# Cross-attention with scores in 32-row groups of heads over four banks, layer norm of x on POOL and a new order of work

## What is computed

```python
x = x + _L0_xattn_ref(_layernorm(x), ctx_1024, ctx_1024, w_q, w_k, w_v, w_o)
...
# each of them, with 16 heads of 8 numbers; scale, bias and mask differ by layer
Q = (query @ w_q.T).reshape(B, L, N_HEADS, D_K).transpose(0, 2, 1, 3)
K = (key @ w_k.T).reshape(B, L, N_HEADS, D_K).transpose(0, 2, 1, 3)
V = (value @ w_v.T).reshape(B, L, N_HEADS, D_K).transpose(0, 2, 1, 3)
scores = jnp.einsum('bhqd,bhkd->bhqk', Q, K) / jnp.sqrt(jnp.float32(D_K))
attn = jax.nn.softmax(scores, axis=-1)
out = jnp.einsum('bhqk,bhkd->bhqd', attn, V)
return out.transpose(0, 2, 1, 3).reshape(B, L, D_MODEL) @ w_o.T
```

## Time and profile before

| | us |
|---|---|
| median of 3 runs | 3282.99 (3280.1 to 3283.28) |
| the profiled execution | 3285.16 |
| its span, first to last instruction | 3283.5 |
| L0 cross-attention, from its first transposes | 27 to 335 |
| L1 cross-attention | 508 to 816 |
| L2 cross-attention | 1233 to 1565 |
| L3 cross-attention | 1669 to 1974 |

### The profile page before, as it was taken

One profiled execution on the slowest core, in us unless ns is written; L12 is line 12 of the kernel. 1 busy time (PEld: TensorE's weight loads), 2 busy tenths in 40 slices (PEclk: granted clock), 3 DMA queues, 4 the chain that ended last, 5 costly groups with the idle time before them and its releaser, 6 DMA issues. The chain is left out here.

```text
span 3283.5 us, 95494 instructions
## 1 busy us (share of the span) xinstructions
PE 3036.9 (92%) x34128; PEld 2065.7 (63%) x34128; DVE 2480.1 (76%) x5721; ACT 1622.4 (49%) x2596; POOL 981.8 (30%) x1128
## 2 busy tenths in 40 slices
PE   5999678998999999999989996999997989999989
PEld 3666565666566656666656664666674656666655
DVE  6888686887677767777568877888885668888756
ACT  3666214565333334555346666666663356666523
POOL 4000000000000000000110005888882268888734
PEclk9999668999999999999899998999998999999999
DMA  4111001111000002111001110000001100000022
GB/s 155 29 30 23 13 0 24 28 30 24 7 0 0 0 5 42 40 40 23 13 20 46 40 41 14 10 10 10 10 3 26 26 14 10 6 10 10 4 77 77
DMA packets 190847, 81.12 MB, mean 25 GB/s; under 512 B 175921, under 2 KB 176496, under 8 KB 190208
## 3 DMA queue, kind: packets, MB, share of 16 engines
q1 hardware_dynamic: 187024, 69.14, 9.1%
q0 software_dynamic: 3696, 10.28, 0.9%
HBM read 37.54 MB, written 8.39 MB: 14 GB/s over the span
## 5 line engine op out<-in xcount | busy, mean ns | idle before, releaser
L864 ACT ACTIVATE probs_t<-ps_pt 128x1024 f32<-128x1024 f32 x256 | 262.2, 1024 | 388.4 <-PE ps_pt L980 388.4
L726 DVE TENSOR_REDUCE row_max<-ps_s 128x16 f32<-128x1024 f32 x256 | 313.2, 1223 | 113.5 <-PE ps_s L969 110.4
L2088 POOL TENSOR_TENSOR kblk<-kblk 128x1024 f32<-128x1024 f32 x128 | 302.1, 2360 | 140.3 <-DVE kblk L2131 140.3
L710 POOL TENSOR_TENSOR x<-x,out_bias_L 128x512 f32 (+1 forms) x32 | 40.6, 1270 | 971.9 <-DVE x_norm L495 500.8
L731 DVE TENSOR_TENSOR probs<-ps_s,row_max 128x1024 f32<-128x1024 f32 x256 | 311.9, 1218 | 11.7
L1002 PE MATMUL ps_o<-v,probs_t 128*64 128x18 f32 x8192 | 285.9, 213 | 5.4 <-issue 5.3
L1002 PEld LDWEIGHTS ps_o<-v,probs_t 128*64 128x64 f32 x8192 | 260.5, 138 | 40.4 <-issue 19.0
L980 PE MATMUL ps_pt<-ident,probs 128*128 128x128 f32 x2048 | 278.1, 279 | 7.2 <-ACT probs L859 7.2
L969 PE MATMUL ps_s<-kblk,q_t 64*64 64x512 f32 x2048 | 273.6, 607 | 5.7 <-issue 5.6
L859 ACT ACTIVATE probs<-probs 128x1024 f32<-128x1024 f32 x256 | 269.6, 1053 | 14.4 <-DVE probs L731 13.0
L1682 POOL TENSOR_TENSOR probs<-probs 128x512 f32<-128x512 f32 x16 | 16.6, 1039 | 860.9 <-ACT probs L1659 860.9
(11 more groups left out here) (334 smaller groups left out, 6823.2 us busy)
## 6 DMA issues: line engine op xcount, KB each, us to landing
ci<-in_ctx_t SPq DMA_DIRECT2D x64, 256.0 KB, 3.0
kblk<-k_t SPq DMA_DIRECT2D x688, 16.0 KB
ci<-x SPq DMA_DIRECT2D x64, 128.0 KB
ci<-x SPq DMA_DIRECT2D x128, 63.0 KB
x<-in_x_in SPq DMA_DIRECT2D x4, 1024.0 KB, 8.7
mask<-in_mask_l SPq DMA_DIRECT2D x64, 64.0 KB, 2.5
out<-x SPq DMA_DIRECT2D x16, 256.0 KB, 2.0
out<-x POOLq DMA_DIRECT2D x16, 256.0 KB, 2.4
```

The costliest lines, as they stand in the source:

```text
L726: dve.tensor_reduce(row_max[u % 2][:, :], scores_of(u), AX, ALU.max).then_inc(max_ready.sem, 1)
L864: act.activation(probs_t[:, :, :], ps_pt[:, :, :].rearrange("p a (r t) -> p (a r) t", t=P), ACT.Copy).then_inc(pt_ready.sem, 1)
L2088: pool.tensor_tensor(a, a, b_, ALU.add).then_inc(rotated.sem, 1)
```

## The change

- **Scores.** RG is 4: four groups of 32 rows (four heads each), eight matmuls of 32x64 with 256 columns for a tile. Row group c writes bank c, so that a tile takes half of each of all four banks, and scores of tile u wait for the shift of tile u - 1. The masks are put in by eight matmuls of 256 columns in place of four of 512, still with 64 rows (MASK_ROWS). maxima and shift read the same 1024 numbers, now out of four banks. kblk is half as long per group of keys; place_keys still has 16 transfers of the same size.
- **Norm.** POOL does a group with two instructions of 128x512 (x - mean, then times 1/deviation); norm_tile is gone from DVE in these stages. POOL's late loads in L0 are issued in portions of five behind each of the first groups.
- **V.** values_even is ACT's too.
- **Order.** The lists of PE, DVE and ACT are written anew.

The core of the diff; the new lists of DVE and ACT and the changed names of kblk are left out:

```diff
-RG = 2
+RG = 4
+MASK_ROWS = P // 2
...
+            score_banks = ps_s[:, :, 0:RH * S]
+            scores_4 = score_banks.rearrange("p c (h k) -> p c h k", k=S)
...
-                    if name == "L0":
-                        for dst, src in late_loads:
-                            pool.dma_start(dst, src).then_inc(loaded_late.sem, 16)
+                    late = late_loads if name == "L0" else []
+                    unrolled = 10 if late else 1
+                    share = (len(late) + unrolled - 1) // unrolled
+                    def normalise_rows(g):
...
+                        wait_past(pool, xt_in_psum, g, 0)
+                        pool.sem_inc(pool_turn.sem, 1)
+                        pool.tensor_tensor(x_norm[:, :, :], rows,
+                                           mean_all[:, bass.ds(g * GT, GT)].unsqueeze(2).broadcast_to(spread),
+                                           ALU.subtract).then_inc(x_norm_ready.sem, 1)
...
+                    for g in range(unrolled):
+                        body(g)
+                        for dst, src in late[g * share:(g + 1) * share]:
+                            pool.dma_start(dst, src).then_inc(loaded_late.sem, 16)
...
-                        wait_past(pe, shifted, g, u - 1)
+                        wait_past(pe, shifted, g, u)
                         pe.sem_inc(pe_turn.sem, 1)
-                        bank = ps_scores[u % 2]
...
                         for c in range(RG):
                             rows = slice(c * RP, (c + 1) * RP)
                             for b in range(2):
                                 tok = slice((2 * u + b) * S, (2 * u + b + 1) * S)
-                                last = pe.matmul(bank[b * S:(b + 1) * S, c, :], q_t[par][rows, tok],
+                                last = pe.matmul(score_banks[b * S:(b + 1) * S, c, :], q_t[par][rows, tok],
                                                  kblk[par][rows, :, tok], start=plain, stop=True,
                                                  skip_group_check=not plain)
```

More of the change, by code:

```diff
@@ L1025, in body @@
                         if soon:
-                            project_v(g + 1, other)
-                            scores(g + 1, 0, other)
+                            scores(g + 1, 0, 1 - par)
+                        if late:
+                            project_k(g + 2, par)
                         if now:
```

151 lines of the change are left out of this document (77 added, 74 removed).

## The result

The changed kernel takes 3232.68 us (median of 4 runs, 3226.7 to 3233.41), the kernel before 3281.76: a ratio of 0.9847, interval 0.983 to 0.9864, or 49 us less. The profiled execution took 3232.17 us with a span of 3230.4. The forecast was 3215 in a range of 3190 to 3262: the sign and the range held, and a quarter of the gain is missing.

The account below looks back on a forecast made before the run. PE was taken to bound each cross-attention stage. From 3285.16, minus 64.5 for groups, plus 5 for starts, minus 8.6 for L0's start gave 3217.1 profiled; the median, 2.2 lower, was 3214.9, rounded 3215; range 3190 to 3262.

Parts of the forecast that it names:

- 64.5 us in the groups: Steady groups of the four cross-attention stages: gains of 1.13 in L0, 1.01 in L1 and L3, 1.17 in L2, over 15 groups.
- The score phase, 0.60 forecast: PE's scores of one tile in L0: 1.02 us becomes 0.60, bounds 0.50 and 1.02; 1.68 us a group.
- The rival that eight do not run together (3299): Only four score matmuls run at once, scores stay at 1.02 us and groups get longer: 3299 us; chance 0.11.
- The form between mask and scores: 0.03 forecast: PE's change of form between mask and scores adds 0.03 us: the two take 0.88 in L1 and L3, 1.55 in L2.
- Tile 2's copy, 0.40 / 0.12 / 0 forecast: PE waits for ACT's copy of tile 2's turned probs: 0.40 us in L0, 0.12 in L1 and L3, nothing in L2.
- the 0.15 a group for small waits: Allowance of 0.15 us a group for small waits, such as project_v on the copy of q_t and turn_probs on ACT.
- "The operations stand end to start": PE's timeline of one group, 203.73 to 221.92, has no idle time, so a us less PE work is a us gained.
- Norm on POOL: DVE loses 1.9 us a group in L0 with norm and V; worth nothing alone, but lets maxima and shift follow scores.
- The +5 for the starts: Later x_norm and scores one tile at a time delay stage starts; 5 us added for the three later stages.
- Start of L0, 8.6 forecast: Late loads in portions: 3.6 us of the 5.62 stall before group 1's scores and 5 from half clock go.
- more than forecast: Rival: scores at 0.50 us and no waits beside tile 2's, 0.45 a group, 20 us more: 3195 us; chance 0.13.

Follow-up runs that it names:

- the run with the mask twice: Changed kernel with the mask's matmuls of L1 and L3 issued twice, the second writing the same values; 3262.9 us, ratio 0.9934.
- the run with the loads alone: Kernel before, with only POOL's late loads issued in ten portions behind the layer norms of L0's first ten groups; 3274.7 us, ratio 0.9977.
- the norm on DVE: Changed kernel with the layer norm of x back on DVE (four norm_tile a group) instead of POOL; 3256.0 us, ratio 0.9917.
- SP's new order: Changed kernel with SP issuing a group's context load before the 16 key transfers, not after them (L2 keeps the old order); 3220.9 us, ratio 0.9817.
- the run with the loop cut: Kernel before, every engine's order kept, PE's loop body ending one operation earlier, between scores of tile 3 and turn_o; 3277.7 us, ratio 0.9984.
- V even on DVE: Changed kernel with the even half of V copied by DVE again, between the statistics of tile 0 and its shift; 3472.1 us, ratio 1.0563.
- the banks alone: Kernel before, with only the scores changed: four 32-row groups over four banks, one tile at a time; 3270.3 us, ratio 0.9966.

## Why the prediction was right, and what was mis-sized

The mechanism held: the scores fell as forecast, and 28 of the 49 us go when they are put back. The total owes something to luck. The forecast gave all of its 64.5 us in the groups to the scores, and they brought 38 on top of the rest of the change; 19 us of the rest, which it had counted at nothing, made up for most of that.

- **The score phase, 0.60 forecast: right.** 0.62 in L0. The rival that eight do not run together (3299) is out. The sum itself did not close: two passes of 0.43, 0.05 and 0.07 make 0.98 for the old phase and not its 1.02. The Trainium skill, TensorE: Matmul & The Clock Gate, section Part 3, gives one matmul's time and about 4 ns for each further tile. Here a further tile costs 7 ns, and the eight start over 0.046 us: the forecast's 0.05, more than the page's 0.03.
- **The form between mask and scores: 0.03 forecast, 0.12 measured** (mask and scores 0.96 for 0.88 and 1.65 for 1.55). The Trainium skill, TensorEngine Tiling (Array Packing), section Tiling Modes, says that a change of mode drains TensorE. The trace agrees so far as such a change costs time, 0.12 in the run with the mask twice. The step that failed had one change of form in the scores' 0.60 already and put only 0.03 on the second one. 4 x 0.09 x 3 stages x 15 = 16 us of the missing gain: the largest term.
- **Tile 2's copy, 0.40 / 0.12 / 0 forecast.** The place was right, the releaser half: scores wait 0.28 for the shift, and only 0.08 behind it is the copy (212.60 to 213.30 for 0.62). In L1 the wait is again 0.28 and not 0.12, since the mask doesn't cover a wait that stands ahead of it; the 0.15 a group for small waits made up for that there.
- **"The operations stand end to start": wrong**, and in the gain's favour. I read the rows of a group and passed over 217.64 with its 0.38 us. That wait is 8 us over the stages; order, norm and V without the scores, it included, were worth 0.49 in L0 and 0.3 in L1 and L3, 19 us with L2 (1.25 x 15), and I had counted nothing for it.
- **A ring on SP, not seen.** The row of SP gave the 10.71 us, and I looked only at the keys' landing. The context behind them holds L0 at 16.6; with it gone 0.43 us a group more is gained there, and 0.17 in L3: 9 us.
- **Norm on POOL.** The prediction said that it is worth nothing alone and that it lets maxima and shift follow the scores. Alone it was never tried. In the changed kernel it is worth 1.44 us in the sum of four groups, 22 us over 15, so the whole does need it, and the sum had no price for that; but the wait that it saves is that of turn_x for the norm, not that of scores for the shift. It takes 1.04 us an instruction, not 1.25. The +5 for the starts was near: from the stages less their 15 groups the four starts and ends cost 5.3 us.
- **Start of L0, 8.6 forecast.** Alone the portions gave 8.0. In the changed kernel the first two groups are 7.0 shorter, of which 2.6 are the steady gain: 4.4. By the length of its operations PE runs at half speed from 42.66 to about 50 there, which the run with the loads alone does not. The first group is 20.1 us with the four banks and SP's old order (also with the norm on DVE and with the mask twice), and 16.9 with two banks or with SP's new order: it takes both.
- **First groups of L2 and L3, not counted.** They became 2.7 and 2.0 us longer while the others got shorter. The first two tiles of L2 were 2.26 us apart and are 5.41 now; one tile's banks leave nothing to do until the shift:

```profile
1207.26 1.98 PE L977 MATMUL ps_s<-mask,ident 64*64 64x256 f32 x16 [2.22 <-DVE probs L755]
1209.18 1.15 PE L988 MATMUL ps_s<-kblk,q_t 32*64 32x256 f32 x16
```

In L2 this first group is 16.3 to 17.5 us in the four runs with two banks, whoever makes the norm, and 19.7 to 21.9 in the ten with four: so it is the banks. In L1 and L3 it is 15.7 to 18.1 with two and 16.7 to 21.7 with four, and the 2.0 of L3 are within what one and the same stage differs by (L1 has 18.1 before and 16.0 in the run with the loads alone).

The account, forecast against measured: steady groups 64.5 and 57.2 (3.81 x 15); L0's start 8.6 and 4.4; first groups of the later stages 0 and -5.7; starts and ends -5 and -5.3. Forecast 68.1, measured 50.6 of the stages' 50.9; with 2.2 elsewhere the profiled executions differ by 53.0. (In the rival *more than forecast* 0.45 a group is 27 us over 60 groups, not 20.)

## What to carry to other kernels

When an operation is shortened, list for each place what it had been covering, and give every stretch its own cover; a tuned order has several chains within 0.3 us of each other, and removing one wait shows the next. Read every row of a group, those with "issue" above all, and look for rings through a DMA queue: the sum of their parts is a floor that no engine's busy share shows. A part that is worth nothing in a sum of busy times (the norm here) can be what another part needs.

## What was not expected of the hardware

- A loop's end costs PE 0.3 to 0.4 us where a single short matmul that has itself been waited for stands before it (before, 217.64 and 585.00), and nothing that shows where the matmuls of one tile's scores do (the run with the loop cut).
- A change of form costs about 0.1 us: turn_o takes 0.26 where weigh_values follows and 0.16 where turn_probs does, scores behind the mask cost 0.12.
- With PE idle for 2.3 us once a group (V even on DVE) the granted clock fell after every second wait, to 0.70 over 28 us, while waits of 0.2 to 0.8 several times a group (the banks alone) left L0 at full speed (the window from 60 to 316 us):

```profile
60.00:316.00 256.00, 233.48 (x3983) 176.66 (x3981) 211.41 (x415) 157.77 (x229) 0.00 (x0) 1.00 0.14 28
```

- At the start of L0 the clock column can be empty and still read 1.00. turn_probs takes 1.97 us there in the changed kernel, twice its time, in a window that reads 1.00 (42.60 to 49.20); but the list of clock levels in this trace begins only at 50.0 us, with full speed. In the run with SP's order it begins at 35.9, and the same 1.97 us (at 43.15) stands in a window at half:

```profile
45.58 1.97 PE L999 MATMUL ps_pt<-ident,probs 128*128 128x128 f32 x8
```

```profile
42.70:45.80 3.10, 3.10 (x22) 2.51 (x18) 2.28 (x4) 0.67 (x2) 0.28 (x1) 0.50 0.14 27
```

  The durations are right. Before, the list begins at 38.0: the first transposes took 1.09 us for 0.65, so PE was at half speed there too, and the 1.00 and 0.98 of the L0 stages in the windows above and in the earlier trace rows leave that out.
